# First heads of an attention stage: one pair's query lows on GpSimd, `p_hi` after each half, two projections' work moved back

## The reference

```python
x = x + 0.5 * ffn(layernorm(x))       # 3 blocks: linear, layernorm, gelu, linear, residual; 4-bit weights + LoRA
x = x + attn(layernorm(x))
x = x + 0.5 * ffn(layernorm(x))       # same weights
# attn, 16 heads of rank 64:
xq = einsum('btd,hrd->bthr', x, Q);  xk = einsum('bud,hrd->buhr', x, K)
scores = einsum('bthr,buhr->bthu', xq, xk) / sqrt(128)
out = einsum('bthu,bud,hde->bte', softmax(scores, axis=3), x, VO)
```

## Time and profile before

| what | value |
|---|---|
| median of 3 runs | 987.42 us (986.22 to 987.95) |
| profiled execution | 987.76 us, of which the span of the profile is 986.0 us |
| PE busy | 956.5 us (97%) |
| DVE busy | 855.1 us (87%) |
| ACT busy | 807.4 us (82%) |
| POOL busy | 829.5 us (84%) |

### The profile page before, as it was taken

How to read it: one execution, slowest core, us unless ns; L and a number is a source line. 1 busy time by engine, 2 the same in 40 slices (tenths; PEclk the granted TensorE clock), 3 DMA queues, 4 the chain that set the end, 5 groups by cost and what they waited for, 6 DMA issues and landing times.

```text
span 986.0 us, 19436 instructions
## 1 busy us (share of the span) xinstructions
PE 956.5 (97%) x6005; PEld 509.7 (52%) x6005; DVE 855.1 (87%) x1741; ACT 807.4 (82%) x1341; POOL 829.5 (84%) x938
## 2 busy tenths in 40 slices
PE   4889899999999999999999999999999999999998
PEld 4668344444444444444444444444444444444777
DVE  7678999999999999999999999999999988986664
ACT  4866788888888888888888888888888988888774
POOL 3645699899998999899999999999999998899552
PEclk9999999999999999999999999999999999999999
DMA  9000322222222222222222222222222222221002
GB/s 253 1 1 9 89 65 65 65 59 68 61 59 62 63 63 59 62 63 65 66 65 65 65 65 65 65 65 57 63 62 61 64 61 61 63 62 33 2 1 86
DMA packets 71744, 59.89 MB, mean 61 GB/s; under 512 B 11168, under 2 KB 70560, under 8 KB 71648
## 3 DMA queue, kind: packets, MB, share of 16 engines
q1 hardware_dynamic: 71392, 58.31, 24.0%
q10 hardware_dynamic: 256, 0.39, 0.2%
HBM read 6.23 MB, written 2.10 MB: 8 GB/s over the span
## 4 chain that ended last, share of the span: by engine, by line
PE 91%; DVE 5%; POOL 2%; issue 1%; DMA 1%; ACT 0%; SPq 0%; POOLq 0%; DVEq 0%; ACTq 0%
PE ps L1219 12%; PE ps L1211 11%; PE ps L1221 11%; PE ps L1220 11%; PE ps L1212 11%; PE ps L1204 7%; PE ps L1195 3%; PE ps L1238 3%; PE ps L1234 3%; PE ps L1235 3%; PE ps L1113 3%; PE ps L1196 3%; PE ps L1197 3%; PE ps L1142 2%; PE ps L1123 1%; PE ps L1154 1%
## 5 line engine op out<-in xcount | busy, mean ns | idle before, releaser
L470 POOL TENSOR_TENSOR p_lo<-work_b,p_hi 128x1024 f16<-128x1024 f32 x256 | 540.1, 2131 | 46.3 <-ACT p_hi L615 45.7
L920 DVE TENSOR_REDUCE mcol<-ps 128x2 f16<-128x1024 f32 x256 | 301.4, 1222 | 2.2 <-PE ps L1204 2.1
L610 ACT ACTIVATE work_b<-ps,exp_scale 128x1024 f32<-128x1024 f32 x256 | 271.5, 1111 | 36.5 <-PE ps L1212 36.3
L615 ACT ACTIVATE p_hi<-work_b 128x1024 f16<-128x1024 f32 x256 | 256.0, 1055 | 0.0
L1211 PE MATMUL ps<-head_ops 128*128 128x512 f16 x512 | 194.1, 379 | 2.9 <-DVE mcol L920 1.5
L1219 PE MATMUL ps<-p_hi,xn_hi 128*128 128x512 f16 x512 | 194.7, 380 | 0.9 <-POOL p_lo L470 0.9
L1220 PE MATMUL ps<-p_hi,xn_lo 128*128 128x512 f16 x512 | 194.0, 379 | 0.0
L1221 PE MATMUL ps<-p_lo,xn_hi 128*128 128x512 f16 x512 | 194.0, 379 | 0.0
L1212 PE MATMUL ps<-head_ops 128*128 128x512 f16 x512 | 194.0, 379 | 0.0
L479 POOL TENSOR_TENSOR x<-x,o_sb 128x512 f32<-128x512 f32 x126 | 160.2, 1271 | 5.4 <-POOL rstd L447 0.2
L931 DVE STREAM_TRANSPOSE head_ops<-mcol 32x128 f16<-32x128 f16 x512 | 155.4, 304 | 9.3
(11 more groups left out here) (139 smaller groups left out, 1378.9 us busy)
## 6 DMA issues: line engine op xcount, KB each, us to landing
head_ops<-pair_ops SPq DMA_DIRECT2D x512, 64.0 KB, 2.0
head_ops<-pair_ops SPq DMA_DIRECT2D x128, 128.0 KB, 2.4
x<-x_dram SPq DMA_DIRECT2D x8, 256.0 KB, 5.9
out<-x SPq DMA_DIRECT2D x8, 256.0 KB, 2.5
vo_last<-wvo_dram SPq DMA_DIRECT2D x1, 1024.0 KB, 11.9
qk<-wq_dram SPq DMA_DIRECT2D x1, 512.0 KB, 5.2
qk<-wk_dram SPq DMA_DIRECT2D x1, 512.0 KB, 6.0
scl<-scales_dram ACTq DMA_DIRECT2D x8, 48.0 KB, 5.3
```

What stands on the lines that cost most here:

```text
L470: pool.tensor_tensor(p_lo[:, k % 2, rows, :], p32[:, k % 2, rows, :], p_hi[:, k % 2, rows, :], ALU.subtract).then_inc(plo_done, 1)
L610: nc.scalar.activation(p32[:, k % 2, 2 * a:2 * a + 2, :], s_ps[a], ACT.Exp, scale=exp_scale[:, 0:1]).then_inc(exp_done, 1)
L615: nc.scalar.activation(p_hi[:, k % 2, 2 * a:2 * a + 2, :], p32[:, k % 2, 2 * a:2 * a + 2, :], ACT.Copy).then_inc(phi_done, 1)
L920: nc.vector.tensor_reduce(mcol[:, pair % 2, :, t, 0], max_ps[pair == 1][t % 2], AX.X, ALU.max, negate=True).then_inc(max_red, 1)
```

## The change

GpSimd computes the query lows of pair 1 instead of DVE. It can't read the PSUM bank, so ACT copies the projection in fp32 to a new tensor `q_full` first. For this GpSimd's `vo_low(1)` moves to the end of head 1's slot, and TensorE waits for it only in slot 9. On ACT, head 0's order becomes exps, p_high, exps, p_high instead of two exps, then two p_highs; y_high(0) moves ahead of k_high(3). On DVE, q_low of pair 2 moves behind the first two reduces of pair 2. On TensorE, maxima(0,2) moves ahead of a `lin2` half, and project_k(3) moves from ahead of slot 1 to behind outputs(0) inside slot 1.

```diff
+        q_full = sb("q_full", [128, T])
+        qfull_ready = sem("qfull_ready")
@@ GpSimd
             xn_low(0, 0)
             xn_low(0, 1)
             vo_low(0)
-            vo_low(1)
+            pool.wait_ge(qfull_ready, 1)
+            pool.wait_ge(qh_ready, 2)
+            pool.wait_ge(ql_ready, 1)
+            pool.tensor_tensor(pair_ops[:, 1, 1, :], q_full[:, :], pair_ops[:, 1, 0, :],
+                               ALU.subtract).then_inc(ql_ready, 1)
@@ GpSimd, slot(k)
                     p_low(k, a)
+                if k == 1:
+                    vo_low(1)
                 late(k)
@@ ACT
             q_high(1, 1)
+            nc.scalar.activation(q_full[:, :], q_ps[1], ACT.Copy).then_inc(qfull_ready, 1)
             nc.scalar.activation(exp_warm[:, :], ident[:, 0:1], ACT.Exp)
             for a in range(2):
                 exps(0, a)
-            for a in range(2):
                 p_high(0, a)
             pair_free(2, 0)
             k_high(2, 0)
@@
             q_high(2, 0)
             for a in range(2):
                 p_high(1, a)
+            y_high(0)
             pair_free(3, 1)
             k_high(3, 1)
-            y_high(0)
@@ DVE
             k_low(1, 1)
-            q_low(1, 1)
             reduce_max(1, 1)
             pair_free(2, 0)
             k_low(2, 0)
             reduce_max(1, 2)
-            q_low(2, 0)
             reduce_max(1, 3)
             row_max(2)
             reduce_max(2, 0)
             reduce_max(2, 1)
+            dve.wait_ge(ql_ready, 2)
+            q_low(2, 0)
             y_low(0)
@@ TensorE, slot(k)
                 if k == 1:
+                    pe.wait_ge(prep_p, 11)
+                    pe.wait_ge(prep_a, 6)
+                if k == H // 2 + 1:
                     pe.wait_ge(prep_p, 12)
-                    pe.wait_ge(prep_a, 6)
                 if k == NH - 1:
                     lin1(1, 0)
                 outputs(k - 1)
+                if k == 1:
+                    project_k(3)
@@ TensorE, ahead of the slots
             maxima(0, 1)
-            lin2(0, STEPS - 1, [0])
             pe.wait_ge(max_red, 1)
             maxima(0, 2)
+            lin2(0, STEPS - 1, [0])
             project_q(1)
@@
             project_k(2)
-            pe.wait_ge(ql_ready, 2)
+            pe.wait_ge(qfull_ready, 1)
+            pe.wait_ge(qh_ready, 2)
             pe.wait_ge(xnl_ready, 2)
             pe.wait_ge(plo_done, 1)
             weigh(0, 0)
@@
                 maxima(2, a)
-            project_k(3)
```

## The result

The changed kernel takes 990.64 us (median of 6 runs, 989.46 to 992.09) against 987.47 (986.00 to 987.95, 6 runs): a ratio of 1.0036, 95% interval 1.0025 to 1.0048, or 2.5 to 4.7 us more. The forecast was 990.0, slower. Its profiled execution took 989.46 us with a span of 987.1.

The account below looks back on a forecast made before the run. TensorE, 91% of the span, was taken to bound the kernel. The moved projection and what queues behind it gave +2.45 us at project_q(3), slot 2 +0.09: +2.54 on 987.42 is 989.96, say 990.0 us, range 989.4 to 990.8.

Parts of the forecast that it names:

- steps 2 and 7: Step 2, maxima(0,2) ahead of lin2: nothing, plus or minus 0.1 us; step 7, slots 2 and 3: only +0.09 us.
- Rival D: Shared SBUF port: row_max(0)'s transposes wait for GpSimd's new instruction, scores(0) up to 1.1 us later, 991.1 us; chance 0.03.
- parts 1 to 3: GpSimd's query lows and earlier maxima(0,2): nothing each; head 0's `p_hi` after each half: scores(2) +0.17 us.
- No more is lost: Slots 2 and 3: scores(3)'s second half +0.09 us, then slot 3's reduces done before they are needed.
- rival C: DVE takes slots to recover, pushing each of the next two by 0.6 to 0.9 us: 991.5 us; chance 0.10.
- the prediction's own signs of being wrong: Head 2's exponentials near 119, scores(2) before 117.3, or distance to before still growing after scores(3).
- Rival A: Head 0's shorter chain starts scores(2) 0.6 us early, total 989.2 us; with the outright null, chance 0.23.
- rival B: Faster: scores(2) 1.2 us early, k_high(3) not holding head 2's exponentials; 985.1 or 986.9 us; chance 0.05.

Follow-up runs that it names:

- h2: Kernel before with lin2(0,3) swapped ahead of `turn_tops` in the first feed-forward pass: 985.55 us, ratio 0.9982.
- e3: Changed kernel with head 0's order on ACT put back (exps, exps, p_high, p_high): scores(2) at 10.71 us against 11.20, scores(3) at 20.65, clock fallen.
- e1: Changed kernel with project_k(3), k_high(3) and q_low(2) put back in their earlier places: scores(1) to scores(3) 18.09 us, +0.66 against the kernel before.
- e6b: Repeat trace of the changed kernel with y_low(0) ahead of q_low(2) on DVE, clock held: scores(1) to scores(3) 19.65 us against 20.01.
- e4: Changed kernel with ACT's k_high(3) moved behind the two exponentials of head 2: scores(1) to scores(3) 20.00 us against 20.01.
- e5: Changed kernel with ACT's k_high(3) behind head 2's exponentials and DVE's k_low(3) behind row_max(3) and output scaling: scores(1) to scores(3) 18.68 us, +1.25 against before.
- f1: Kernel before with GpSimd making query lows of pairs 1 and 2 and maxima(0,2) earlier: 987.31 us against 987.60, ratio 0.9999.
- r1: Changed kernel timed and traced again, nothing altered: 990.56 us against 987.60, ratio 1.0035; scores(1) to scores(3) 21.15 us with the clock fallen.
- e6: Changed kernel with y_low(0) ahead of q_low(2) on DVE, first trace, clock fallen: scores(1) to scores(3) 21.15 us.
- h1: Kernel before with GpSimd's query lows of pairs 1 and 2, maxima(0,2) earlier, and lin2(0,3) swapped ahead of `turn_tops`: 985.13 us against 987.31, ratio 0.9979.

## Why the prediction was right

The measured 990.64 lies 0.64 over the forecast and inside its range, and the mechanism was the one forecast, with two terms mis-sized (steps 2 and 7). Step by step, positions counted from scores(1) and moved to the axis of the earlier trace rows by adding 2.09 to those of after:

1. GpSimd's query lows cost nothing. The instruction took 1.16 (1.1 expected), `q_full` 0.59 with 1.38 us of ACT's waiting left behind it. Rival D, the shared port, falls: the transposes of row_max(0) under it took 1.26, as the others, and scores(0) started 1.32 us after row_max(0) (100.85 to 102.17) against 1.31 before (102.94 to 104.25). The warning in the Trainium skill, "Perfetto Trace Analysis", section "Optimizing Scalar/DVE Operations", did not come true for these instructions.
2. maxima(0,2): it gained about 0.17, where the sum had nothing, with a bound of 0.1. From the transposition in which both traces are still alike (96.42 before, 94.51 after) to row_max(0) it is 6.52 before and 6.34 after, and 6.34 or 6.35 in all ten other traces with this part against 6.51 in h2, which lacks it. The prediction held reduce(0,3) to be bound to TensorE's maxima(0,3); before, it stood directly behind reduce(0,2), which waited 0.78 for its own maxima. DVE, before and then after:

```profile
97.13 1.22 DVE L920 TENSOR_REDUCE mcol<-ps 128x2 f16<-128x1024 f32 x1
98.53 1.23 DVE L920 TENSOR_REDUCE mcol<-ps 128x2 f16<-128x1024 f32 x1 [0.18 <-PE ps L1204]
100.54 2.36 DVE L920 TENSOR_REDUCE mcol<-ps 128x2 f16<-128x1024 f32 x2 [0.78 <-PE ps L1204]
```
```profile
95.21 1.22 DVE L928 TENSOR_REDUCE mcol<-ps 128x2 f16<-128x1024 f32 x1
96.62 2.36 DVE L928 TENSOR_REDUCE mcol<-ps 128x2 f16<-128x1024 f32 x2 [0.18 <-PE ps L1212]
99.59 1.23 DVE L928 TENSOR_REDUCE mcol<-ps 128x2 f16<-128x1024 f32 x1 [0.61 <-PE ps L1212]
100.85 1.26 DVE L939 STREAM_TRANSPOSE head_ops<-mcol 32x128 f16<-32x128 f16 x4
```

3. The interleaved `p_hi`: the second half of scores(1) at 108.59 (108.60 expected), maxima(1,1) at 109.56 (109.56), project_q(2) at 112.30 (112.25), scores(2) at 118.06 (117.98). e3 shows by undoing it that the order costs 0.49 to scores(2); DVE's two instructions less win back 0.24 of that (10.71 in e3 against 10.95 before). With `q_low(2)` back in its old place, parts 1 to 3 lose 0.66 (e1).
4. q_low(2) ahead of y_low(0): the third matmul of outputs(0) at 120.43 (120.29). Turning the two round wins 0.36 (e6b), against 0.28 in the sum.
5. project_k(3) at 121.00 to 121.65 (120.86 to 121.51): 0.65.
6. What is queued behind it: exponentials of head 2 at 122.43 (122.29), project_q(3) at 124.92 (124.79), that is +2.58 against +2.45. The two waits ahead of the maxima are 1.09 together, where some 1.3 were expected. Here the prediction named ACT's queue as the cause, and that was half of it: e4 shows that freeing ACT alone is worth nothing, as DVE holds the same projection's copy ahead of its row maxima. The sum had both times in it (k_low(3) to 123.12, reduces to 127.63), but the text priced only one.
7. "No more is lost" was the step that was mis-sized: 0.09 was given to slots 2 and 3, and they lost 0.44 (+2.58 at scores(3), +2.89 at scores(4), +3.03 at scores(5), +3.02 at scores(6)). The second half of scores(3) waits for a reduce and `y_low(1)` comes late to outputs(1); e5, where DVE is not late, has the loss constant from scores(3) on (+1.25, +1.25, +1.26, +1.25). That was rival C's mechanism, at under a third of its price, and it is one of the prediction's own signs of being wrong: the distance to before still grew after scores(3). Nor is it constant after scores(6): in two later slots the matmul that waits for `y_low` comes 0.1 us later than before, so that the distance is +3.13 from scores(52) on and +3.22 from scores(98) to the last. e1 has the same two steps (+0.66, +0.76, +0.86). What makes `y_low` late there stays open.

So the sum over the traces is 3.02 - 0.17 + 0.20 = 3.05 us instead of 2.54. The medians are 3.17 apart, and the ratio gives 2.5 to 4.7. That they come this near is partly luck: the clock falls at `turn_tops` in some executions of either kernel, for 1.7 us, and behind the longer wait of the changed one in some, for 1.1 more, of which the prediction had nothing; which executions the median falls on decides as much as the terms that were mis-sized. Rival A fails, as scores(2) is later and not earlier; rival B fails, as `k_high(3)` ended at 120.44 of the trace of after, 2.4 us behind the last matmul of scores(2).

## What to carry to other kernels

Moving a producer later moves everything that is queued behind its consumers: here a 0.65 us projection cost 1.3 to 1.8 us more, as two engines had its copies at the head of their queues, and taking it from ACT's alone gained nothing. Measure a local edit from an event ahead of all of it in the same trace: the two spans differed by 1.1 us where the edit cost 3.0, and even scores(1), which lies behind two of the edits here, hid 0.17. Then follow the distance to the end, as a local gain can shrink (0.62 to 0.30 in f1). Where one wait on TensorE is long, bring ready work into it: one swap in a place that the change never touched won 1.8 us (0.9 to 2.7).

## What the runs showed of the hardware

In these traces TensorE's granted clock falls from its full level (2.4 GHz, 1.00) to the lower one (1.2 GHz, 0.50) behind a wait of 2.0 to 2.6 us in some executions of the same program and not in others. Ahead of `turn_tops` (wait of 2.49 to 2.64 us) it fell in 7 of 11 traces without the swap (the group of four fp32 matmuls behind it took 2.55 to 3.57 us instead of 1.88); ahead of scores(2) (2.03 to 2.04 us) in 3 of 7, for 1.1 us in r1 and 1.5 us in e6. Behind waits of 0.6 to 1.7 us at these two places it held in all. A third place, which no experiment touched, agrees: ahead of a group of transpositions near 28 us of each trace it fell in all eight traces with a wait of 3.57 to 3.64 us and in none of the five in which TensorE came later and waited 1.43 to 1.93. That the wait brings the fall is argued from these counts; the swap at `turn_tops` tests it, with a timing clear of noise. The 22 runs of the kernel before beside h1 show two heaps, 985.95 to 986.73 and 987.27 to 988.22, with one at 988.86. The mean granted clock of a run goes with them: 0.998 or more in 8 of the 9 lower ones and in 1 of the 13 higher ones, and in all 22 runs of h1 and h2. So some 1.4 us between two runs of one kernel can hang on it.
